# Deformable layer: 13 groups of shifts, five pair sums merged on GpSimd, eight projections, and the far-event chain laid on other shifts

## The chip, the cores and the metric

The kernel is one program on one NeuronCore of a Trainium2 chip. The metric is the device time of one execution in microseconds. The engines are TensorE (PE, with its weight loads PEld), VectorE (DVE), ScalarE (ACT), GpSimd (POOL) and SyncE (SP), which issues most DMAs. They run side by side and meet at semaphores.

## The reference, cut to what matters

The input is x, (4, 128, 64, 64) in float32. A deformable convolution layer is followed by a Mamba block, an attention and expert layer, a second attention and a last expert layer. Only the first layer is touched. It computes:

```
val = xf @ w_value + b_value                       # xf: group-normed x, P = 4096 pixels, C = 128
om  = (xf @ w_off + b_off).reshape(N, P, G=8, 32)  # 9 taps: offsets y, x and a mask
for the four corners of each sample point:
    acc += gather(val, corner) * weight(corner) * valid(corner)
out = (acc * mask).sum(over 9 taps) @ w_out + b_out
out = batchnorm(out);  x += out * sigmoid(out)
```

An offset may point anywhere. Most are small: a sample point then lies within one pixel of its tap, so the gather is a sum over 25 shifts (dy, dx in -2 to 2) of the value image, each with a weight that is a product of two hat functions. The few points beyond ("far events", up to 128 in an image) are found, gathered and added by themselves.

## The kernel before

`deform_near` (L146) works in 16 units: four images (b = 0 to 3) times four units of 8 rows in each half image. A tile is 128 x 1024 (two halves of 512 pixels). In each unit t runs over the 25 shifts, which fall in 9 classes (a class has one product of a y hat and an x hat).

- GpSimd multiplies hats by the mask (`mask_hat`, L378) and forms the tap weights of a class (L426) in a ring of 5 slots. A slot is free when the last shift of its old class is spread. It also adds the finished unit to x (`add_out`, L384) and issues the indirect DMAs of the far events (L393, L399).
- TensorE spreads the tap weights of shift k over the channels (`spread_shift`, L859: four 36x64 matmuls, shown as 8) into one of three PSUM pairs. Behind some shifts it puts other items in the same ring (`prepared`): "o" offsets of unit U + 4 (L808), "v" values (L817), "c" steps of the far-event chain (L823 to L848).
- VectorE multiplies the pair by the shifted values (`product`, L495). The first product of a group goes to SBUF (`near_weighted`, three places), the others stay in PSUM and are added to it (`add`, L506). Groups have 3, 3, 3, 3, 3, 3, 3, 2 and 2 shifts: 25 products, 16 additions, 9 projections.
- TensorE projects a finished group with w_out into `near_out_sum` (L879), two shifts behind the group's last. Ahead of a unit's last projection stands the event pair (L871). The first product of a group waits until the group three before it is projected.
- ScalarE evaluates the offsets (L660, L661), the values (`keep_values`, L673), the hats of the next unit (L694 to L712, at t = 14), and the gate (`bn_gate`, L730) once the last projection of a unit is done. It runs its items in order, the gate first.
- VectorE also finds the largest offsets of unit U + 4 (`find_far`, L514 to L517, at t = 17), and carries the chain: `rank_far` (L521 to L528), `select_far` (L534 to L539), `locate`, `corners` (L557 to L577), `gather_sum`, `event_values`. In the last unit of an image it ranks and selects for the next, in the first unit it does the rest.
- SyncE spills offsets to DRAM and reloads them in the order in which its code is written.

The order on every engine is the order of the code; nothing reorders it. A wait holds everything behind it on its engine.

## Time and profile before

| | |
|---|---|
| median of 3 runs | 7284.67 us (7283.68 to 7285.45) |
| profiled execution | 7285.44 us, span 7283.6 us |
| busy in the span | PE 5758.8, PEld 2032.5, DVE 5812.3, ACT 5316.8, POOL 1443.2 us |
| the layer at hand | from about 50 us to 1165 us, 16 units |
| mean granted TensorE clock | 0.918 of full speed |

### The profile page before, as it was taken

How to read it: one execution, taken by the hardware profiler on the slowest of the kernel's cores; microseconds unless marked ns; L12 is line 12 of the kernel's file. 1: busy time of each engine (PE TensorE's matmuls, PEld its weight loads, DVE VectorE, ACT ScalarE, POOL GpSimd, SP SyncE). 2: the span in 40 equal slices, each digit the busy share in tenths (PEclk: the TensorE clock that was granted, in tenths of full speed). 3: DMA queues.
4: the chain of work that ended last, by engine and by line, in shares of the span. 5: the costliest groups of instructions: out<-in, count | busy, mean ns of one | idle time of the engine just before them, and what ended most of it. 6: DMA issues, size and time to landing. Idle time of an engine off the chain costs nothing. (4 is left out here: it accounts for less than half of the span.)

```text
span 7283.6 us, 89413 instructions
## 1 busy us (share of the span) xinstructions
PE 5758.8 (79%) x32962; PEld 2032.5 (28%) x32962; DVE 5812.3 (80%) x12374; ACT 5316.8 (73%) x3820; POOL 1443.2 (20%) x1695
## 2 busy tenths in 40 slices
PE   7887886788769998977767777887778787778787
PEld 2222222344324443422211222222222222222223
DVE  7888887676557765888777788989889898889996
ACT  3333322455545553579999999999999999999996
POOL 3444441000136654620000000000000000000002
PEclk7888987888879998989999999999999999999998
DMA  3111100100000000000000000000000000000000
GB/s 120 53 42 48 53 19 11 30 24 24 12 9 1 1 1 4 1 7 1 1 1 1 1 1 1 1 1 1 12 1 1 1 1 12 1 1 1 1 1 24
DMA packets 45167, 95.26 MB, mean 13 GB/s; under 512 B 7863, under 2 KB 9657, under 8 KB 43578
## 3 DMA queue, kind: packets, MB, share of 16 engines
q1 hardware_dynamic: 43834, 88.43, 3.7%
q8 instruction: 267, 4.37, 0.2%
q0 software_dynamic: 896, 1.06, 0.1%
q14 instruction: 170, 1.39, 0.1%
HBM read 39.13 MB, written 33.55 MB: 10 GB/s over the span
## 5 line engine op out<-in xcount | busy, mean ns | idle before, releaser
L2814 ACT ACTIVATE aa_tanh<-aa_tanh 128x4096 f32<-128x4096 f32 (+5 forms) x1120 | 3671.0, 3367 | 24.0 <-DVE aa_tanh L2994 23.9
L2994 DVE TENSOR_SCALAR aa_tanh<-aa_f_times,aa_g_bias 128x1024 f32<-128x1024 f32 (+18 forms) x5120 | 2983.2, 643 | 476.6 <-PE aa_scores L2860 470.5
L2860 PE MATMUL aa_scores<-aa_tanh,aa_w_spread 128*32 128x512 f32 (+8 forms) x18432 | 2164.8, 583 | 808.3 <-ACT aa_tanh L2814 803.9
L2860 PEld LDWEIGHTS aa_scores<-aa_tanh,aa_w_spread 128*32 128x32 f32 x18432 | 581.0, 112 | 2237.0 <-ACT aa_tanh L2814 1119.6
L2874 PE MATMUL aa_out_sum<-aa_weights,aa_normed 128*128 128x512 f32 (+3 forms) x1152 | 640.7, 640 | 60.4 <-DVE aa_weights L3003 57.7
L2782 POOL TENSOR_SCALAR aa_group_normed<-x_rows,norm_scale,aa_shift_plus 128x128 f32<-128x128 f32 x96 | 93.2, 982 | 2411.2 <-PE aa_turned L2901 1766.7
L859 PE MATMUL near_weights_spread<-near_tap_weights,near_spread_consts 36*64 36x512 f32 x3200 | 442.6, 664 | 76.4 <-DVE near_weighted L506 36.4
L2085 PE MATMUL qa_out<-qa_hidden_rows,qa_weights_in 128*128 128x512 f32 x1024 | 475.4, 607 | 0.0
L495 DVE TENSOR_TENSOR near_weights_spread<-near_weights_spread,near_values 128x1024 f32<-128x1024 f32 x256 | 314.1, 1227 | 109.7 <-PE near_weights_spread L859 109.0
L879 PE MATMUL near_out_sum<-near_weighted,near_w_out 128*128 128x512 f32 x576 | 342.0, 724 | 65.8 <-DVE near_weighted L506 65.4
L426 POOL TENSOR_TENSOR near_tap_weights<-near_hat_y_mask,near_hat_x 128x1024 f32<-128x1024 f32 x144 | 339.6, 2372 | 197.4 <-PE near_weights_spread L859 137.9
L2806 ACT ACTIVATE aa_weights<-aa_scores,aa_weights_in 128x1024 f32<-128x1024 f32 (+5 forms) x320 | 312.8, 977 | 89.5 <-PE aa_scores L2860 89.5
L2770 POOL TENSOR_SCALAR aa_normed<-x_rows,norm_scale,aa_attention_shift_plus 128x128 f32<-128x128 f32 x128 | 101.1, 806 | 1162.5 <-PE aa_out_sum L2874 1154.6
L2874 PEld LDWEIGHTS aa_out_sum<-aa_weights,aa_normed 128*128 128x128 f32 x1152 | 182.7, 199 | 524.2 <-issue 416.7
L506 DVE TENSOR_TENSOR near_weighted<-near_weighted,near_weights_spread 128x1024 f32<-128x1024 f32 x256 | 312.7, 1221 | 17.0 <-DVE near_weights_spread L495 0.5
L2447 ACT ACTIVATE L_ffn_weighted<-L_ffn_experts,L_ffn_gates 128x128 f32<-128x128 f32 x640 | 182.8, 369 | 162.2 <-PE L_ffn_experts L2403 161.7
L2037 ACT ACTIVATE qa_hidden_rows<-qa_hidden 128x512 f32<-128x512 f32 x320 | 170.0, 595 | 153.3 <-PE qa_hidden L2076 153.3
L2544 DVE SCALAR_TENSOR_TENSOR x_rows<-L_ffn_experts,L_ffn_gates,x_rows 128x128 f32<-128x128 f32 x640 | 216.8, 346 | 70.8 <-PE L_ffn_experts L2403 59.2
L2403 PE MATMUL L_ffn_experts<-L_ffn_expert_w_centred,L_ffn_normed_T 128*128 128x512 f32 x512 | 250.4, 617 | 20.4 <-DVE x_rows L2544 13.4
L3104 DVE SCALAR_TENSOR_TENSOR x_rows<-aa_turned,aa_gates,x_rows 128x128 f32<-128x128 f32 x768 | 264.0, 344 | 0.0
L2085 PEld LDWEIGHTS qa_out<-qa_hidden_rows,qa_weights_in 128*128 128x128 f32 x1024 | 184.8, 190 | 282.4 <-issue 282.4
L730 ACT ACTIVATE near_bn_out<-near_out_sum,near_bn_shift,near_bn_scale 128x1024 f32<-128x1024 f32 x16 | 19.3, 1205 | 301.3 <-PE near_out_sum L879 301.3
(434 smaller groups left out, 6799.8 us busy)
## 6 DMA issues: line engine op xcount, KB each, us to landing
near_offsets<-near_offset_staged SPq DMA_DIRECT2D x45, 512.0 KB, 3.1
l_taps<-l_scan_in_out SPq DMA_DIRECT2D x256, 64.0 KB, 2.0
x_rows<-in_x SPq DMA_DIRECT2D x4, 2048.0 KB, 15.9
near_offset_y<-near_offsets SPq DMA_DIRECT2D x15, 512.0 KB, 4.1
near_offset_x<-near_offsets SPq DMA_DIRECT2D x15, 512.0 KB
near_mask<-near_offsets SPq DMA_DIRECT2D x15, 512.0 KB, 5.5
out_x<-x_rows SPq DMA_DIRECT2D x3, 2048.0 KB, 6.3
out_x<-x_rows SPq DMA_DIRECT2D x8, 256.0 KB, 2.0
```

The lines of the kernel that those rows point to most:

```text
L426: pool.tensor_tensor(PP[:, n % PR_, :], HY[:, cy, :], HX[:, cx, :], ALU.mult).then_inc(p_ready, 1)
L495: v.tensor_tensor(out.rearrange("p s (r w) -> p s r w", w=WW), w.rearrange("p s (r w) -> p s r w", w=WW), V[:, :, at:at + 8 * VW].rearrang ...
L506: v.tensor_tensor(PR[:, at, :], PR[:, at, :], wp[:, PAIR["s", U, t] % 3, :, :].rearrange("p s n -> p (s n)"), ALU.add).then_inc(added, 1)
L859: last = t.matmul(wp[o:o + 64, r, s, :], e[64 * h:64 * h + 36, :], PP[64 * h:64 * h + 36, n % PR_, s * BANK:(s + 1) * BANK], start=True, s ...
L879: last = t.matmul(acc[:, s, :], WO2[:, s, :], PR[:, gi % 3, s * BANK:(s + 1) * BANK], start=g == 0, stop=g == NGR - 1)
L2085: last = t_.matmul(fo[:, n % 2, :], W2T[:, SET * q + g, :], HR[:, q % 2, g, :], start=q == 0 and g == 0, stop=q == NQ - 1 and g == SET - 1)
L2806: a.activation(ET[:, n % 2, 0:w], sp_[:, n % 2, 0:w], ACT.Exp, bias=B2C).then_inc(e_ready, 1)
L2814: a.activation(TH[:, u % PLACES, 0:length], TH[:, u % PLACES, 0:length], ACT.Tanh).then_inc(th_ready, 1)
L2860: last = t.matmul(sp_[32 * q:32 * q + 32, n % 2, s:e], W2S[:, tt, :], TH[:, p, o + s:o + e], start=tt == 0, stop=tt == 3, tile_position=(0 ...
L2874: last = t.matmul(op[:, s0:(h + 1) * BANK], UN[:, j * P:(j + 1) * P], ET[:, n % 2, s0 - lo:(h + 1) * BANK - lo], start=j == 0, stop=n == c ...
L2994: ins = v.tensor_scalar(TH[:, p, at[q]:at[q] + w - s], FR[:, m % 2, lo + s:CHUNK], GB[:, key:key + 1], None, ALU.add)
L3104: v.scalar_tensor_tensor(x, bank("e", E)[:, e * P:(e + 1) * P], GT_[:, G % 2, c:c + 1], x, ALU.mult, ALU.add).then_inc(sum_step if e < 3 e ...
```

## The change

- Groups: `SIZES` is 1 and twelve times 2. 25 products, 12 additions. `near_weighted` has five places (`NSUM`).
- GpSimd adds the sums of the groups (0,1), (2,3), (4,5), (6,7) and (8,9) pairwise (`merge`). Each pair sum has one projection, groups 10, 11 and 12 one each: eight. They stand behind the shifts `PROJECT_AT` = 8, 12, 16, 20, 24, 26, 27, 28, where 26 to 28 are shifts 1 to 3 of the next unit.
- GpSimd's code now runs over t. A class product is put where its slot comes free, four slots ahead (ring of 4 for 5), so that of the next unit's classes the first four are formed in this unit.
- One mask buffer for two; the mask of the next unit is reloaded by itself (`reload_mask`), ahead of the spills.
- Offsets of U + 4 at t = 6, 8, 10 (9, 11, 13 before), values at t = 2 and 4 (5 and 7), find_far at t = 12 (17), hats at t = 11 (14). Chain: rank 13, select 19 (18, 20), locate 1, corners 7, gather_sum 13, event_values 21 (0, 4, 8, 14).
- find_far drops its cast; rank_far reads the indices as they are and uses scalar_tensor_tensor forms for tensor_scalar ones.

```
-        SIZES = [3] * 7 + [2, 2]
+        SIZES = [1] + [2] * 12
         NGR = len(SIZES)
+        PROJECTED = [(0, 1), (2, 3), (4, 5), (6, 7), (8, 9), (10,), (11,), (12,)]
+        PROJECT_AT = [8, 12, 16, 20, 24, 26, 27, 28]
+        NPJ = len(PROJECTED)
+        MERGES = [z for z in PROJECTED if len(z) == 2]
+        MERGE_AT = [5, 9, 13, 17, 21]
...
+            def merge(U, m):
+                g0, g1 = MERGES[m]
+                group_added(pool, U, g0)
+                group_added(pool, U, g1)
+                at, frm = (U * NGR + g0) % NSUM, (U * NGR + g1) % NSUM
+                pool.tensor_tensor(PR[:, at, :], PR[:, at, :], PR[:, frm, :], ALU.add).then_inc(merged, 1)
...
+            for n in range(PR_):
+                class_product(n)
             for U in range(NU):
+                for t in range(NSH):
+                    if t in CLS_LAST and U * NCC + CLS_LAST.index(t) + PR_ < NU * NCC:
+                        class_product(U * NCC + CLS_LAST.index(t) + PR_)
+                    if U and t == 3:
                         add_out(U - 1)
...
+                    if U and U % 4 == 0 and t == 4:
                         gather_offsets(U // 4)
...
+                    if t in MERGE_AT:
+                        merge(U, MERGE_AT.index(t))
...
-                if first and gi >= 3:
-                    v.wait_ge(proj, 1 + gi - 3 + 1)
+                if first and gi >= NSUM:
+                    v.wait_ge(proj, 1 + projection_of(gi - NSUM) + 1)
...
-            CHAIN_FIRST = {11: rank_far, 13: select_far, 16: locate, 18: corners, 21: gather_sum, 24: event_values}
-            CHAIN_BEFORE = {18: rank_far, 20: select_far}
-            CHAIN_WITHIN = {0: locate, 4: corners, 8: gather_sum, 14: event_values}
+            CHAIN_FIRST = {9: rank_far, 12: select_far, 15: locate, 18: corners, 21: gather_sum, 24: event_values}
+            CHAIN_BEFORE = {13: rank_far, 19: select_far}
+            CHAIN_WITHIN = {1: locate, 7: corners, 13: gather_sum, 21: event_values}
...
-                    if t == 17 and U + 4 < NU:
+                    if t == (16 if U == 0 else 12) and U + 4 < NU:
                         find_far(U + 4)
...
-            def project(U, g):
+            def project(U, i):
...
+                if len(z) == 2:
+                    t.wait_ge(merged, 1 + U * len(MERGES) + MERGES.index(z) + 1)
                 else:
+                    group_added(t, U, z[0])
```

TensorE at the start of unit 6, before: shifts 0 and 1 of the unit, the event pair and the last projection of unit 5, shifts 2 to 4, the first projection of unit 6.

```order
L859 MATMUL near_weights_spread<-near_tap_weights,near_spread_consts 64x512 [waits near_product_ready,near_tap_weights_ready]
L859 MATMUL near_weights_spread<-near_tap_weights,near_spread_consts 64x512 x3
L871 MATMUL near_out_sum<-near_event_at,near_event_out 128x512 [waits near_event_at_ready,near_prep_used]
L871 MATMUL near_out_sum<-near_event_at,near_event_out 128x512
L879 MATMUL near_out_sum<-near_weighted,near_w_out_2 128x512 [waits near_sum_added]
L879 MATMUL near_out_sum<-near_weighted,near_w_out_2 128x512
L859 MATMUL near_weights_spread<-near_tap_weights,near_spread_consts 64x512 [waits near_sum_added,near_tap_weights_ready]
```

The same place after: from shift 2 of unit 6 to shift 4. The projections of groups 11 and 12 of unit 5 stand behind shifts 2 and 3.

```order
L899 MATMUL near_weights_spread<-near_tap_weights,near_spread_consts 64x512 [waits near_sum_added,near_tap_weights_ready]
L899 MATMUL near_weights_spread<-near_tap_weights,near_spread_consts 64x512 x3
L918 MATMUL near_out_sum<-near_weighted,near_w_out_2 128x512 [waits near_sum_added]
L918 MATMUL near_out_sum<-near_weighted,near_w_out_2 128x512
L857 MATMUL near_weights_spread<-x_rows,near_w_value_scaled 128x512 [waits near_product_ready,near_weights_scaled]
L857 MATMUL near_weights_spread<-x_rows,near_w_value_scaled 128x512
L899 MATMUL near_weights_spread<-near_tap_weights,near_spread_consts 64x512 [waits near_product_ready,near_tap_weights_ready]
L899 MATMUL near_weights_spread<-near_tap_weights,near_spread_consts 64x512 x3
L910 MATMUL near_out_sum<-near_event_at,near_event_out 128x512 [waits near_event_at_ready,near_prep_used]
L910 MATMUL near_out_sum<-near_event_at,near_event_out 128x512
L918 MATMUL near_out_sum<-near_weighted,near_w_out_2 128x512 [waits near_sum_added]
L918 MATMUL near_out_sum<-near_weighted,near_w_out_2 128x512
```

The last projection moved two shifts later, and the value pair (behind shift 5 before) stands ahead of it.

GpSimd in unit 5, before: `add_out` among the class products 5 and 6 to 8.

```order
L426 TENSOR_TENSOR near_tap_weights<-near_hat_y_mask,near_hat_x 128x1024 [waits near_spread_done,near_hat_y_masked]
L384 TENSOR_TENSOR x_rows<-x_rows,near_bn_out 128x2x512 [waits near_y_ready]
L426 TENSOR_TENSOR near_tap_weights<-near_hat_y_mask,near_hat_x 128x1024 [waits near_spread_done,near_hat_y_masked] x3
L378 TENSOR_TENSOR near_hat_y_mask<-near_hat_y_mask,near_mask 128x1024 [waits near_hat_y_ready,near_mask_loaded_0]
```

After, in an ordinary unit: `add_out`, the last mask product of the unit, class product 6, the first merge (L446), class product 7, the second merge.

```order
L410 TENSOR_TENSOR x_rows<-x_rows,near_bn_out 128x2x512 [waits near_y_ready]
L404 TENSOR_TENSOR near_hat_y_mask<-near_hat_y_mask,near_mask 128x1024 [waits near_hat_y_ready,near_mask_loaded]
L438 TENSOR_TENSOR near_tap_weights<-near_hat_y_mask,near_hat_x 128x1024 [waits near_spread_done,near_hat_y_masked]
L446 TENSOR_TENSOR near_weighted<-near_weighted 128x1024 [waits near_sum_added,near_product_ready]
L438 TENSOR_TENSOR near_tap_weights<-near_hat_y_mask,near_hat_x 128x1024 [waits near_spread_done,near_hat_y_masked]
L446 TENSOR_TENSOR near_weighted<-near_weighted 128x1024 [waits near_sum_added]
```

The first merge stands three instructions behind one that waits for the gate.

TensorE behind shift 8 of unit 6, after: the first projection waits for the merge (`near_sums_merged`), the second offset pair and shift 9 stand behind it.

```order
L899 MATMUL near_weights_spread<-near_tap_weights,near_spread_consts 64x512 x3
L918 MATMUL near_out_sum<-near_weighted,near_w_out_2 128x512 [waits near_y_ready,near_sums_merged]
L918 MATMUL near_out_sum<-near_weighted,near_w_out_2 128x512
L848 MATMUL near_weights_spread<-x_rows,near_w_off_scaled 128x512 [waits near_prep_used,near_weights_scaled]
L848 MATMUL near_weights_spread<-x_rows,near_w_off_scaled 128x512
L899 MATMUL near_weights_spread<-near_tap_weights,near_spread_consts 64x512 [waits near_product_ready,near_tap_weights_ready]
```

Before, the projection at this place waited for an addition of VectorE two shifts back.

## Rows read from the trace of the kernel before

**Rows 1.** Windows view: units 5 to 8 and 13, and the stage.
```profile
core 0: us, PE busy (x) PEld busy (x) DVE busy (x) ACT busy (x) POOL busy (x), PEclk, DMA share, GB/s
...
447.00:512.10 65.10, 58.38 (x260) 17.50 (x256) 52.94 (x47) 22.02 (x23) 32.16 (x14) 0.87 0.14 49
512.10:573.80 61.70, 55.20 (x260) 16.71 (x256) 52.87 (x47) 22.13 (x23) 28.63 (x13) 0.92 0.16 52
573.80:649.80 76.00, 62.42 (x290) 22.04 (x286) 64.16 (x57) 22.50 (x25) 29.82 (x13) 0.84 0.12 42
649.80:726.90 77.10, 58.62 (x272) 19.54 (x268) 65.46 (x83) 24.42 (x30) 37.50 (x21) 0.87 0.17 45
...
997.00:1052.50 55.50, 47.47 (x244) 14.38 (x240) 48.59 (x44) 15.51 (x16) 30.82 (x14) 0.91 0.09 29
...
50.50:1165.00 1114.50, 939.73 (x4252) 305.01 (x4252) 935.06 (x928) 343.94 (x381) 506.08 (x234) 0.87 0.14 44
```

**Rows 2.** Timeline of VectorE, units 6 and 7: start us, us, instruction, [idle before, releaser].
```profile
554.11 1.22 DVE L514 TENSOR_TENSOR near_offset_size<-near_offset_size,near_event_at 128x1024 f32<-128x1024 f32 x1
...
558.24 1.21 DVE L495 TENSOR_TENSOR near_weighted<-near_weights_spread,near_values 128x1024 f32<-128x1024 f32 x1
...
579.23 1.23 DVE L495 TENSOR_TENSOR near_weights_spread<-near_weights_spread,near_values 128x1024 f32<-128x1024 f32 x1 [1.82 <-PE near_weights_spread L859]
...
582.84 1.22 DVE L495 TENSOR_TENSOR near_weights_spread<-near_weights_spread,near_values 128x1024 f32<-128x1024 f32 x1
584.09 1.22 DVE L506 TENSOR_TENSOR near_weighted<-near_weighted,near_weights_spread 128x1024 f32<-128x1024 f32 x1
585.23 1.23 DVE L495 TENSOR_TENSOR near_weights_spread<-near_weights_spread,near_values 128x1024 f32<-128x1024 f32 x1
```

**Rows 3.** Timeline of TensorE in unit 6.
```profile
542.67 1.88 PE L808 MATMUL near_weights_spread<-x_rows,near_w_off_scaled 128*128 128x512 f32 x4
544.48 2.81 PE L859 MATMUL near_weights_spread<-near_tap_weights,near_spread_consts 36*64 36x512 f32 x24
...
554.25 1.98 PE L879 MATMUL near_out_sum<-near_weighted,near_w_out 128*128 128x512 f32 x4 [1.28 <-DVE near_weighted L506]
...
559.60 1.98 PE L859 MATMUL near_weights_spread<-near_tap_weights,near_spread_consts 36*64 36x512 f32 x8 [2.35 <-DVE near_weighted L495]
...
564.37 3.78 PE L879 MATMUL near_out_sum<-near_weighted,near_w_out 128*128 128x512 f32 x4 [0.39 <-DVE near_weighted L506]
```

**Rows 4.** Timelines of GpSimd and ScalarE in unit 7.
```profile
578.18 1.20 ACT L730 ACTIVATE near_bn_out<-near_out_sum,near_bn_shift,near_bn_scale 128x1024 f32<-128x1024 f32 x1 [17.35 <-PE near_out_sum L879]
...
579.46 2.35 POOL L384 TENSOR_TENSOR x_rows<-x_rows,near_bn_out 128x1024 f32<-128x1024 f32 x1 [1.56 <-ACT near_bn_out L730]
581.77 4.67 POOL L426 TENSOR_TENSOR near_tap_weights<-near_hat_y_mask,near_hat_x 128x1024 f32<-128x1024 f32 x2
...
586.88 1.27 ACT L673 ACTIVATE near_values<-near_weights_spread,near_bias_cols 128x512 f32<-128x512 f32 x2 [7.49 <-PE near_weights_spread L817]
```

**Rows 5.** Windows view, 559.4 to 569.6 in unit 6 (columns as in rows 1).
```profile
559.40:569.60 10.20, 9.20 (x28) 2.39 (x32) 8.27 (x8) 1.40 (x2) 8.16 (x4) 0.50 0.33 98
```

**Rows 6.** Timelines in unit 7 (rank_far) and unit 8 (corners).
```profile
621.06 1.27 DVE L521 TENSOR_SCALAR near_far_is<-near_far_top 128x12 f32<-128x12 f32 x1
622.36 2.26 DVE L523 TENSOR_SCALAR near_far_missed<-near_far_top 128x4 f32<-128x4 f32 x1
...
626.95 0.17 DVE L525 TENSOR_TENSOR near_far_at<-near_far_at,near_far_half 128x12 f32<-128x12 f32 x1
...
627.79 0.59 PE L823 MATMUL near_weights_spread<-near_far_number,consts_sb 128*128 128x1 f32 x2 [9.87 <-DVE near_far_number L528]
...
661.26 4.40 DVE L557 TENSOR_TENSOR near_event_sample<-near_event_base,near_event_offset 128x2 f32<-128x2 f32 x1
```

**Rows 7.** GpSimd's timeline in unit 8; the page's list of DMA issues.
```profile
654.14 0.94 POOL L393 DMA_INDIRECT near_event_offset<-near_offsets,near_event_offset_rows  x1 [0.31 <-issue]
...
near_mask<-near_offsets SPq DMA_DIRECT2D x15, 512.0 KB, 5.5
```

More of the change, by code:

```diff
@@ L246, in adds_until, with projection_of, group_added @@
             return U * (NSH - NGR) + t - group_of(t)
+        def projection_of(gi):
+            U, g = divmod(gi, NGR)
+            return U * NPJ + [g in z for z in PROJECTED].index(True)
+        def group_added(eng, U, g):
+            S = U * NSH + G_FIRST[g + 1] - 1
+            if SIZES[g] > 1:
+                eng.wait_ge(added, 1 + adds_until(S))
+            else:
+                eng.wait_ge(prod, 1 + S + 1)
         def pieces(U):
@@ L271, in prepared @@
                 items.append(("b", 1))
-            if t in (9, 11, 13) and U + 4 < NU:
-                items.append(("o", U + 4, KINDS[(t - 9) // 2]))
-            v = (15, 18) if U == 0 else (5, 7)
+            ahead = (10, 12, 14) if U == 0 else (6, 8, 10)
+            if t in ahead and U + 4 < NU:
+                items.append(("o", U + 4, KINDS[ahead.index(t)]))
+            v = (16, 19) if U == 0 else (2, 4)
             if t in v and v.index(t) < len(pieces(U)):
@@ L277, in prepared @@
             b, u = divmod(U, 4)
-            if u == 3 and b + 1 < NB and t in (19, 23):
-                items.append(("c", b + 1, (19, 23).index(t)))
-            c = (12, 15, 22, 23, 24) if U == 0 else (-1, -1, 10, 12, 16)
+            if u == 3 and b + 1 < NB and t in (17, 23):
+                items.append(("c", b + 1, (17, 23).index(t)))
+            c = (11, 15, 22, 23, 24) if U == 0 else (-1, -1, 16, 19, 24)
             if u == 0 and t in c:
@@ L333, in spill_unit, with reload_offsets @@
                         sp.dma_start(parked[b][kind, :, :, u, :], halves(STG[:, k % 2, :])).then_inc(spilled[k % 2], 16)
-            def reload_unit(U):
+            def reload_offsets(U):
                 b, u = divmod(U, 4)
-                for kind in KINDS:
+                for kind in KINDS[:2]:
                     spills_done(sp, U, kind)
@@ L354, in _ @@
             for U in range(NU):
+                if U and U + 1 < NU:
+                    reload_mask(U + 1)
                 if U + 4 < NU:
@@ L402, in _ @@
+            def merge(U, m):
[6 more added lines that the diff above has]
+                class_product(n)
             for U in range(NU):
-                for cls in range(NCC):
-                    if U and cls == 6:
+                for t in range(NSH):
+                    if t in CLS_LAST and U * NCC + CLS_LAST.index(t) + PR_ < NU * NCC:
+                        class_product(U * NCC + CLS_LAST.index(t) + PR_)
+                    if U and t == 3:
@@ L493, in product @@
                 w = wp[:, PAIR["s", U, t] % 3, :, :]
-                out = PR[:, gi % 3, :].rearrange("p (s n) -> p s n", s=2) if first else w
+                out = PR[:, gi % NSUM, :].rearrange("p (s n) -> p s n", s=2) if first else w
                 v.tensor_tensor(out.rearrange("p s (r w) -> p s r w", w=WW), w.rearrange("p s (r w) -> p s r w", w=WW),
@@ L763, in _ @@
                             keep_bias(1, 1, NB)
-                    if t == 14 and U + 1 < NU:
+                    if t == (14 if U == 0 else 11) and U + 1 < NU:
                         hats_y(U + 1)
@@ L912, in _ @@
                             bias_columns(1, 1, NB)
-            project_if_last(NU * NSH - 2)
-            project_if_last(NU * NSH - 1)
+            for k in range(5):
+                projections_at(NU, k)
 def deform_wide(nc, d, X, consts):
```

116 lines of the change are left out of this document (57 added, 59 removed).

## The prediction, made before the changed kernel was run

> **What bounds the kernel now.** First the windows view, one window for the whole stage and some for single units. The stage, from the first product of unit 0 to the end, is 1114.5 us of the 7283.6 us span; VectorE is busy for 935 and TensorE for 940 of it, GpSimd for 506 [rows 1]. All else in the program is untouched, so the change is worth what it does to the 16 units. An ordinary unit (6 is one) lasts 61.7 us, a unit that ranks far events (7) 76.0, the one that gathers them (8) 77.1, a unit without offsets to prepare (13) 55.5 [rows 1]. Then the timeline of unit 6 by engine. On VectorE a product that opens a group occupies 1.14 us until the next instruction, a product 1.25 and its addition 1.14 (582.84, 584.09, 585.23), which makes 2.39 for the two [rows 2]. On TensorE a shift costs 0.95 (24 matmuls, three shifts, in 2.81) and a projection, an offset pair or a value pair about 1.85 (542.67 to 544.48) [rows 3]. In unit 6 VectorE works 9 x 1.14 + 16 x 2.39 + 3.9 for find_far (554.11 to 558.24 less a little overlap) = 52.4 us, of 61.7: so some 9 us are waits, and these have TensorE as their releaser, such as the 1.82 at 579.23 [rows 2]. TensorE's side shows why: it waits, 1.28 us at 554.25, for the last addition of a group before it projects it, then needs 1.85 + 0.95 before VectorE has a shift again [rows 3]. With an offset pair between, VectorE runs dry. So neither engine bounds alone; they hand three PSUM pairs back and forth, and the projection lies in that loop.
>
> **The change, part by part.** 13 groups for 9: 13 opening products, 12 additions, in place of 9 and 16. VectorE loses 4 x 1.25 us a unit (an opening product pays 1.14 for the 2.39), so 5.0 us a unit, 80 us over 16 units, if it bounded alone. The 0.37 us cast after find_far goes (558.24 shows that 0.3 of it counts) [rows 2]. TensorE loses one projection, 1.85 us. GpSimd gets 5 merges of 2.31 us, the pitch of its 128x1024 tensor_tensor (579.46 to 581.77) [rows 4], 11.6 us a unit, on top of 28.6 in a unit of 61.7 [rows 1]: 40 of about 60, so it does not bound by its sum. The five sum places give a slot back before VectorE comes to it, since product t waits for a projection that stands on TensorE's queue ahead of shift t anyway. The class products of the next unit now start at t = 14 with hats begun at t = 11; I cost that, and four class slots for five, at nothing: a class product is issued at least 6 shifts ahead of its use. The single mask buffer is covered too: SyncE sends the mask of the next unit once mask_hat of t = 4 is done, ahead of the spills in its queue, it lands 5.5 us later [rows 7], and is wanted at t = 14; the offset pairs keep their distance of two shifts, some 4 us or more. If that cover went, GpSimd would hold class products, not TensorE at once.
>
> What is late next is found by walking one unit. Let T be the end of the last projection of the unit before, which now stands behind shift 3. Ahead of T TensorE has bunched work: projections behind shifts 24, 1, 2, 3, the event pair, a value pair. Shift 1 needs the pair that product 23 frees, so it ends 1.3 us before product 0 starts; then 1.85 (projection), 0.95, 3.7 (projection, values), 0.95, 3.7 (event pair, projection): T is 9.8 us after product 0. VectorE waits 1.4 us for shift 3 and 3.5 for shift 4 (ready at T + 0.95).
> Behind T on the other engines: the gate ends at T + 1.2, and only then ScalarE empties the value pair, 1.27 us [rows 4], so shift 5 starts at T + 2.6; GpSimd starts add_out at T + 1.3 (578.18 to 579.46), and behind it in its queue stand mask_hat, class product 6 and the first merge, so the merge starts at T + 1.3 + 3 x 2.31 = 8.2 and ends at T + 10.6. TensorE has shifts 5, 6, an offset pair, 7 and 8 done at T + 8.2, where the first projection waits for that merge: 2.5 us. Everything behind it on TensorE's queue waits too: projection 12.5, offset pair 14.4, shift 9 at T + 15.3. VectorE had ended shift 8 at T + 10.8: 4.5 us dry. Then product 9, 10 to T + 18.9, 11 (0.6 late), 12, find_far 3.7: product 13 at T + 26.7. From there on four shifts cost TensorE 4 x 0.95 + 1.85 = 5.65 and VectorE 7.06, VectorE bounds, 6 x 3.53 = 21.2. Next product 0 at T + 47.9, so the unit is 57.7 us.
> During find_far TensorE runs out of pairs: it idles about 3 us (before: 1.28 and 2.35, and then the clock is at 0.50 of full speed, a shift costs 1.98 and a projection 3.78 [rows 3, 5]). I take it to fall again: four shifts then cost 4 x 1.85 + 3.7 = 11.1 us on TensorE against 7.06; over 10.2 us at 0.50 that is up to 3.6, less the lead of the ring, 2.5 taken. Ordinary unit: about 60 us, 1.7 less than now.
>
> The units with a chain gain more. In unit 7 rank_far is 6.7 us (621.06 until TensorE starts at 627.79) because three of its operations on 12 elements or fewer last 1.27, 2.26 and as long again, back to back, the length of a GpSimd instruction; the one at 626.95 takes 0.17; and TensorE, which has the pair for `ranked` at the head of its queue, idles 9.87 us [rows 6]. After the change rank_far is at t = 13 and the pair at 17, so TensorE does not reach it first; GpSimd waits for the hats at that time, so I take 3 us for rank_far (bounds 1.3 and 7). 57.7 + 3 + 5 (select_far, unchanged) + 3.3 for the lower clock = 69: 7 less. The Trainium skill, page "SBUF — State Buffer", section "Who interferes with whom", says that a VectorE instruction with two SBUF inputs contends with a GpSimd instruction that reads SBUF, and that GpSimd's side is an exclusive lock. It speaks against the new scalar_tensor_tensor forms, which have two SBUF inputs, and against find_far's first operation now that GpSimd has more to do; the rows agree for small operations (4.40 us for 128x2 [rows 6]).
> In unit 8 corners waits up to 4.4 us now; at t = 7 it lies in front of the 4.5 us wait and hides most of itself, but three indirect DMAs (1.3 us apart [rows 7]) stand ahead of the merge, + 3.2; gather_sum and event_values 2.4, three pairs of the chain and the second value pair 2, lower clock 3: 57.7 + 10.6 = 68.3, 8.8 less.
>
> The sum over units, now less then (units not shown are like the shown ones of their kind, but for 0, 1, 12 and 15, the ends, where I take the additions' 5.0 us and a little from the chain): unit 0, 6; 1, 5; ordinary 2, 6, 9, 10, 1.7 each, 7; 5 (a longer low clock now), 4; 3, 7, 11, 7 each, 21; 4 and 8, 17; 12, 7.5; 13 to 15, which have no offset pairs, by the same walk 51.5, so 4, 1 and 5, together 10. That is 77.5 us. Profiled execution 7285.4 us, 0.8 above the median of 7284.7: 7284.7 - 77.5 = 7207 us.
>
> **The rivals.** A: the clock stays up through find_far and the waits. For it: the idle of 1.28 us leaves it at 1.0, the projection behind it takes 1.98 [rows 3]. Then every unit gains 2.5 more: 7207 - 38 = 7169 us.
> B: it falls behind the wait for the merge as well. The idle there is 2.5 us, about the 2.35 behind which it fell in unit 6 [rows 3], but that one came close behind another. The projection, an offset pair and a shift then cost 3.7, 3.7, 1.9 for 4.6 in all: 4.7 us a unit, 15 units, 7277 us; half of them, 7242. The Trainium skill, "TensorE: Matmul & The Clock Gate", section "The HAM clock gate", calls the throttled state the default which activity lifts; by that rule B and the next are the danger.
> C, the other side: the low clock spreads over TensorE's bunched stretch from shift 1 to shift 10 (20 us of dense work at 1.0, and TensorE bounds there, where before it had slack nearly everywhere), because waits for `merged` and for the value pair keep breaking it. Two spells of 10.2 us, 5 us each, on top of the 60: 7207 + 15 x 9.7 = 7352 us. It decides from 5.2 us a unit upward. Against it: the dense stretch itself recovered the clock in 10.2 us in unit 6.
> D: GpSimd's extra 11.6 us of work a unit holds VectorE's two-input operations. At most 2.3 us for find_far and 7 for each rank_far and corners: 35 + 21 us, half of it taken, 7235 us. Below nothing it cannot be.
> E, that the change does not do what it says, is out for the work: 12 additions and 8 projections stand in the program's order. But the gain can vanish where TensorE bounds; that is B and C.
>
> **Chances.** Forecast 0.45, A 0.20, B 0.16, C 0.08, D 0.11. A measurement tells 0.2% from nothing, 14.6 us, so faster is below 7270: the forecast, A, D and a good half of B, 0.85; B's worse half 0.07; C 0.08. The likeliest one's own range is 7185 to 7230; the range over the cases 7160 to 7262.
>
> **What would show it.** Right: an ordinary unit of 58 to 61 us; VectorE's work in it 47; L446 on GpSimd 80 times at 2.35; TensorE idle 2 to 3 us before the first projection of a unit with the merge as releaser, and VectorE dry for 4 us before product 9; no 9.87 us idle for the rank; VectorE without waits from t = 13 on but for a spell at 0.50. Wrong: units of 62 or more with the granted clock below 0.87 (B, C); product or addition longer than 1.23 us; find_far's L514 well above 1.3 us (D); GpSimd late for shift 5 or 7.

## The result, and the profile after

The change made the kernel slower: 7354.47 us, median of 4 runs (7349.02 to 7358.66), against 7285.06 (7283.68 to 7291.20) for the kernel before. The ratio is 1.0092, 95% interval 1.0079 to 1.0105. The forecast was 7207 us, so it missed by 147 us and on the wrong side. The profiled execution has a span of 7347.2 us against 7283.6, at a mean granted clock of 0.913 (0.918 before).

Measured from VectorE's first product of a unit to the next one's, the 16 units sum to 1169.2 us (1108.3 before). So 61 of the 64 us of the span lie in the stage. By unit (us; unit 15 up to its last product):

| unit | 0 | 1 | 2 | 3 | 4 | 5 | 6 | 7 | 8 | 9 | 10 | 11 | 12 | 13 | 14 | 15 |
|---|---|---|---|---|---|---|---|---|---|---|---|---|---|---|---|---|
| before | 112.8 | 68.8 | 61.7 | 76.1 | 77.1 | 65.1 | 61.6 | 76.1 | 77.1 | 62.0 | 61.5 | 76.1 | 70.5 | 55.5 | 52.3 | 54.0 |
| after | 114.4 | 63.4 | 62.2 | 79.4 | 84.7 | 67.4 | 62.2 | 79.3 | 84.7 | 67.4 | 62.1 | 79.3 | 82.7 | 59.7 | 68.5 | 51.8 |
| forecast | 106.8 | 63.8 | 60 | 69 | 68.3 | 61.1 | 60 | 69 | 68.3 | 60.3 | 59.8 | 69 | 63 | 51.5 | 51.3 | 49 |

Units 1, 2, 6 and 10 are near the forecast. In all the units exceed it by 139 us: 84 in the units with the chain (3, 4, 7, 8, 11, 12), 17 in unit 14, 13 in units 5 and 9, 8 each in units 0 and 13, 9 in the rest. So most of the loss is in the chain units and in unit 14.

Windows view of the kernel after: units 5, 6, 7, 8, 13, 14, then the stage. It answers to [rows 1].

```profile
core 0: us, PE busy (x) PEld busy (x) DVE busy (x) ACT busy (x) POOL busy (x), PEclk, DMA share, GB/s
454.10:521.50 67.40, 59.85 (x256) 18.75 (x260) 47.71 (x42) 21.80 (x23) 41.84 (x18) 0.81 0.14 47
521.50:583.70 62.20, 55.00 (x256) 17.00 (x252) 47.54 (x41) 21.91 (x23) 42.49 (x18) 0.89 0.15 51
583.70:662.90 79.20, 62.60 (x286) 23.62 (x282) 58.51 (x52) 22.39 (x25) 42.43 (x18) 0.81 0.12 40
662.90:747.70 84.80, 62.68 (x264) 20.32 (x256) 67.58 (x78) 24.41 (x30) 49.39 (x26) 0.81 0.14 41
1039.20:1098.90 59.70, 51.40 (x240) 14.98 (x244) 43.86 (x39) 15.51 (x16) 42.09 (x18) 0.79 0.09 27
1098.90:1167.40 68.50, 49.07 (x246) 14.84 (x239) 43.58 (x38) 15.51 (x16) 43.74 (x20) 0.80 0.03 8
49.90:1229.00 1179.10, 956.63 (x4188) 314.96 (x4188) 878.84 (x849) 342.26 (x381) 696.38 (x315) 0.81 0.13 42
```

VectorE's work in an ordinary unit fell from 52.9 to 47.5 us, as forecast, but the unit did not get shorter. All of the 5.3 us became waiting. In unit 8 VectorE is busy longer than before (67.6 against 65.5) though it has fewer instructions: some of them are being held. Over the stage VectorE's busy time fell by 56 us, where the 64 additions and the 15 casts that are gone took 93; the other 37 went into operations that last longer now, find_far's first and small ones of the chain. The line view (busy, mean ns; idle before and its releasers) names the new link:

```profile
L918 PE MATMUL near_out_sum<-near_weighted,near_w_out 128*128 128x512 f32 x512 | 320.5, 759 | 38.1 <-POOL near_weighted L446 38.1
L535 DVE TENSOR_TENSOR near_weights_spread<-near_weights_spread,near_values 128x1024 f32<-128x1024 f32 x192 | 235.2, 1225 | 100.6 <-PE near_weights_spread L899 100.3
L446 POOL TENSOR_TENSOR near_weighted<-near_weighted 128x1024 f32<-128x1024 f32 x80 | 188.6, 2358 | 34.4 <-DVE near_weighted L546 27.1 <-issue 7.2
```

TensorE now waits 38 us for GpSimd's merges, less than the 139 that are missing: the rest has to be found elsewhere. The products themselves are as fast as before (1.22 us).

**Unit 14**: timeline of GpSimd, TensorE and VectorE (start, us, engine, instruction, [idle before, releaser]).

```profile
1119.89 2.34 POOL L438 TENSOR_TENSOR near_tap_weights<-near_hat_y_mask,near_hat_x 128x1024 f32<-128x1024 f32 x1
1127.89 0.38 POOL L466 PARTITION_ALL_REDUCE near_far_max_all<-near_far_max  x1 [5.65 <-PE near_weights_spread L899]
...
1135.50 2.33 POOL L446 TENSOR_TENSOR near_weighted<-near_weighted 128x1024 f32<-128x1024 f32 x1 [7.23 <-issue]
...
1137.88 3.78 PE L918 MATMUL near_out_sum<-near_weighted,near_w_out 128*128 128x512 f32 x4 [9.77 <-POOL near_weighted L446]
...
1143.13 1.23 DVE L535 TENSOR_TENSOR near_weighted<-near_weights_spread,near_values 128x1024 f32<-128x1024 f32 x1 [10.33 <-PE near_weights_spread L899]
```

The all-reduce of the flag is recorded with 0.38 us, but GpSimd does nothing else from 1122.2 to 1135.5, 13.3 us. The profile puts the 5.65 us ahead of it down to TensorE; in the kernel before the same idle time (5.63 us) stands there with no releaser, and the same 13.3 us pass from one instruction to the next (1062.8 to 1076.1):

```profile
1060.46 2.36 POOL L426 TENSOR_TENSOR near_tap_weights<-near_hat_y_mask,near_hat_x 128x1024 f32<-128x1024 f32 x1
1068.46 0.38 POOL L416 PARTITION_ALL_REDUCE near_far_max_all<-near_far_max  x1 [5.63 <-issue]
1076.12 4.67 POOL L426 TENSOR_TENSOR near_tap_weights<-near_hat_y_mask,near_hat_x 128x1024 f32<-128x1024 f32 x2 [7.29 <-issue]
```

After the change a merge stands behind it, TensorE's projection waits for the merge, and VectorE waits for the shift behind the projection. In the old kernel only class products stood behind it, and those have slots in reserve: unit 14 took 52.3 us.

**Unit 6**: timeline of GpSimd, then of TensorE, the front of the unit; it answers to the walk and to [rows 3, 4].

```profile
534.84 2.36 POOL L410 TENSOR_TENSOR x_rows<-x_rows,near_bn_out 128x1024 f32<-128x1024 f32 x1 [7.07 <-ACT near_bn_out L770]
537.15 2.36 POOL L404 TENSOR_TENSOR near_hat_y_mask<-near_hat_y_mask,near_mask 128x1024 f32<-128x1024 f32 x1
539.59 2.35 POOL L438 TENSOR_TENSOR near_tap_weights<-near_hat_y_mask,near_hat_x 128x1024 f32<-128x1024 f32 x1
541.90 2.36 POOL L446 TENSOR_TENSOR near_weighted<-near_weighted 128x1024 f32<-128x1024 f32 x1
```

```profile
531.64 1.88 PE L918 MATMUL near_out_sum<-near_weighted,near_w_out 128*128 128x512 f32 x4
533.45 1.09 PE L899 MATMUL near_weights_spread<-near_tap_weights,near_spread_consts 36*64 36x512 f32 x8
536.07 1.95 PE L899 MATMUL near_weights_spread<-near_tap_weights,near_spread_consts 36*64 36x512 f32 x16 [1.53 <-ACT near_values L713]
537.94 3.67 PE L848 MATMUL near_weights_spread<-x_rows,near_w_off_scaled 128*128 128x512 f32 x4
...
544.32 1.98 PE L918 MATMUL near_out_sum<-near_weighted,near_w_out 128*128 128x512 f32 x4 [0.83 <-POOL near_weighted L446]
```

The order of events is the one that the prediction walked through: gate, add_out, mask, class product, merge, projection. T, the end of the last projection of unit 5, is 533.4, so 11.8 us after product 0 (9.8 forecast). The merge starts at T + 8.5 (8.2 forecast) and ends at T + 10.9 (10.6). GpSimd had stood idle for 7.07 us in front of this, waiting for the gate. TensorE waits only 0.83 us for the merge (2.5 forecast), because the offset pair ahead of it took 3.67 us in place of 1.85: the granted clock is 0.50 from 538.1 to 541.5. VectorE is dry for 2.79 us before product 9 (4.5 forecast).

**Unit 7**: timelines of VectorE, then GpSimd, then TensorE and VectorE again; it answers to [rows 6].

```profile
624.09 0.16 DVE L562 SCALAR_TENSOR_TENSOR near_far_missed<-near_far_top 128x4 f32<-128x4 f32 x1
...
636.10 1.10 DVE L574 SCALAR_TENSOR_TENSOR near_far_number<-near_far_rank,near_far_base,near_far_is 128x12 f32<-128x12 f32 x1
637.24 2.27 DVE L575 TENSOR_SCALAR near_far_missed<-near_far_number 128x12 f32<-128x12 f32 x1
639.54 3.85 DVE L578 TENSOR_TENSOR near_event_rows<-near_spread_consts,near_far_number 128x1536 f32<-128x1536 f32 x1
643.42 2.73 DVE L579 TENSOR_REDUCE near_event_row<-near_event_rows 128x128 f32<-128x1536 f32 x1
```

```profile
634.82 2.35 POOL L438 TENSOR_TENSOR near_tap_weights<-near_hat_y_mask,near_hat_x 128x1024 f32<-128x1024 f32 x1 [1.88 <-PE near_weights_spread L899]
637.14 2.34 POOL L446 TENSOR_TENSOR near_weighted<-near_weighted 128x1024 f32<-128x1024 f32 x1
639.44 2.33 POOL L404 TENSOR_TENSOR near_hat_y_mask<-near_hat_y_mask,near_mask 128x1024 f32<-128x1024 f32 x1
```

```profile
648.69 1.99 PE L899 MATMUL near_weights_spread<-near_tap_weights,near_spread_consts 36*64 36x512 f32 x8 [10.27 <-DVE near_weighted L546]
650.61 5.28 PE L869 MATMUL near_weights_spread<-near_far_at,near_event_rows 128*128 128x1 f32 x24
...
658.93 1.23 DVE L535 TENSOR_TENSOR near_weights_spread<-near_weights_spread,near_values 128x1024 f32<-128x1024 f32 x1 [5.72 <-PE near_weights_spread L899]
```

rank_far is short now: its first operation takes 0.16 us, and the next product follows 0.93 us after it began. But select_far is held. L574 ends at 637.20, L575 at 639.51, L578 at 643.39; the first two end within 0.03 us of the end of a GpSimd instruction, the third 1.6 us after one, which is nearly its own length. In the kernel before, the same three took 0.23, 0.17 and 1.76 us. Meanwhile TensorE runs out of PSUM pairs, idles 10.27 us, comes back at 0.5 of full speed (eight matmuls of a shift in 1.99 us) with 24 matmuls of the chain in hand, and VectorE is dry for 5.72 us.

### The profile page after: what moved, and what is told of

It reads as the page before. It is cut to its first block and busy times, and to the rows that moved or that the text cites. A ratio compares the mean times of both kernels' runs of the same rounds, so it can differ in the third digit from the quotient of the medians.

```text
span 7347.2 us, 89313 instructions
## 1 busy us (share of the span) xinstructions
PE 5759.6 (78%) x32898; PEld 2039.5 (28%) x32898; DVE 5756.4 (78%) x12294; ACT 5315.4 (72%) x3820; POOL 1622.7 (22%) x1775
## 5 line engine op out<-in xcount | busy, mean ns | idle before, releaser
L899 PE MATMUL near_weights_spread<-near_tap_weights,near_spread_consts 36*64 36x512 f32 x3200 | 458.4, 683 | 150.6 <-DVE near_weighted L546 77.4
L535 DVE TENSOR_TENSOR near_weighted<-near_weights_spread,near_values 128x1024 f32<-128x1024 f32 x208 | 252.7, 1220 | 168.7 <-PE near_weights_spread L899 168.2
L918 PE MATMUL near_out_sum<-near_weighted,near_w_out 128*128 128x512 f32 x512 | 320.5, 759 | 38.1 <-POOL near_weighted L446 38.1
L535 DVE TENSOR_TENSOR near_weights_spread<-near_weights_spread,near_values 128x1024 f32<-128x1024 f32 x192 | 235.2, 1225 | 100.6 <-PE near_weights_spread L899 100.3
L2444 PE MATMUL L_ffn_experts<-L_ffn_expert_w_centred,L_ffn_normed_T 128*128 128x512 f32 x512 | 250.7, 618 | 20.3 <-DVE x_rows L2585 13.2
```

The source lines that it names most:

```text
L535: v.tensor_tensor(out.rearrange("p s (r w) -> p s r w", w=WW), w.rearrange("p s (r w) -> p s r w", w=WW), V[:, :, at:at + 8 * VW].rearrang ...
L899: last = t.matmul(wp[o:o + 64, r, s, :], e[64 * h:64 * h + 36, :], PP[64 * h:64 * h + 36, n % PR_, s * BANK:(s + 1) * BANK], start=True, s ...
L918: last = t.matmul(acc[:, s, :], WO2[:, s, :], PR[:, (U * NGR + z[0]) % NSUM, s * BANK:(s + 1) * BANK], start=i == 0, stop=i == NPJ - 1)
L2444: last = t_.matmul(ep[:, t % 2, h, :], UT[:, t // CK % 2, t % CK // 4, (t % 4) * P:(t % 4 + 1) * P], EWC[:, 4 * h:4 * h + 4, :].rearrange( ...
```

## The experiments

The ratio of each is against the kernel before in the same session; the changed kernel itself stands at 1.0092.

**The all-reduce of the flag, out of the way of a merge.**

```
-                    if U == NU - 2 and t == 7:
+                    if U == NU - 1 and t == 22:
```

> The changed kernel with GpSimd's partition_all_reduce (for the far flag) moved from unit 14, t = 7, to unit 15, t = 22. Theory Q (GpSimd's queue: what stands ahead of a merge there is paid by TensorE): in unit 14 TensorE waits 9.77 us for the merge behind it, VectorE 10.33; unit 14 falls from 68.5 to about 57, the whole from 7354 to about 7342 us. Theory C (the low clock on TensorE's bunched stretch is what costs): unit 14 changes by under 4 us.

7341.52 us, ratio 1.0083 (1.0065 to 1.0102). Unit 14 falls from 68.5 to 55.4 us, 13.1 us, as long as GpSimd stood still there. All others stay within 0.1 but for unit 15, which is 3.1 us longer (54.9). 10 us by the trace; the interval of the times alone would not resolve it.

**add_out behind the first merge.**

```
-                    if U and t == 3:
-                        add_out(U - 1)
...
+                    if U and t == 5:
+                        add_out(U - 1)
```

> The changed kernel with add_out moved on GpSimd from t = 3 to behind the first merge (t = 5), so that the first merge no longer stands behind an instruction that waits for the gate. Theory Q: the wait before product 9 (step from product 8 to 9: 5.27 us in unit 6, 2.9 of it wait) goes, 2.5 us in 13 units: about 7320 us. Theory C: TensorE bounds the front half of a unit anyway by its bunched items, so the wait reappears elsewhere: under 10 us less, 7345 or more.

7308.05 us, ratio 1.0036 (1.0022 to 1.0051): 0.56% gained, about 41 us, the most that any single edit of the changed kernel gave. TensorE's wait for merges fell from 38.1 to 20.3 us, unit 6 from 62.2 to 58.0, unit 5 from 67.4 to 62.3. In unit 6 product 9, the first behind the wait for the merge, starts 25.1 us after product 0, where it took 27.6 (521.62 to 549.18) in the changed kernel:

```profile
510.28 2.35 DVE L535 TENSOR_TENSOR near_weighted<-near_weights_spread,near_values 128x1024 f32<-128x1024 f32 x2
...
535.40 1.23 DVE L535 TENSOR_TENSOR near_weighted<-near_weights_spread,near_values 128x1024 f32<-128x1024 f32 x1 [1.89 <-PE near_weights_spread L899]
```

That is 2.4 of the 4.2 us. Another 1.5 is won between products 16 and 17, where the spell at half clock is 3.4 us long in place of 6.8. So an instruction that waits for ScalarE's gate, put ahead of the merge, was dear; part of what the edit gave may have come by way of the clock (0.84 over the stage for 0.81), and the runs do not part the two.

**The old places, with the merges kept.** Offset and value pairs, find_far, hats and chain at their old shifts, and GpSimd's indirect DMAs two and four shifts earlier to fit (the code is cut):

```
-            CHAIN_BEFORE = {13: rank_far, 19: select_far}
-            CHAIN_WITHIN = {1: locate, 7: corners, 13: gather_sum, 21: event_values}
+            CHAIN_BEFORE = {18: rank_far, 20: select_far}
+            CHAIN_WITHIN = {0: locate, 4: corners, 8: gather_sum, 14: event_values}
...
-                    if t == (16 if U == 0 else 12) and U + 4 < NU:
+                    if t == 17 and U + 4 < NU:
```

> The changed kernel (13 groups, merges, eight projections, new order of GpSimd) with the places of before for the offset, value and chain pairs, find_far, the chain's steps on VectorE and the hats; the indirect DMAs one or two steps earlier on GpSimd to fit. Theory P (the places are at fault: the chain's steps now meet GpSimd's merges and empty the ring): units 7 and 8 come back from 79.3 and 84.7 to at most 77, the whole to about 7290 or below. Theory M (groups and merges are at fault wherever the rest stands): 7340 or more.

7415.98 us, ratio 1.0186 (1.0169 to 1.0203). Much worse: the theory that the new places cost the time fell. The line view of this kernel:

```profile
L918 PE MATMUL near_out_sum<-near_weighted,near_w_out 128*128 128x512 f32 x512 | 327.5, 774 | 118.0 <-POOL near_weighted L446 117.9
```

TensorE waits 118 us for merges. GpSimd waits 126 us for the hats of y in front of its mask products (36.5 in the changed kernel), and the merges stand behind these. The new places are what makes the merges bearable; which of them does it, this run does not say, as all moved at once.

**The new places alone, on the kernel before.** The same edit the other way round, without the moves on GpSimd.

> The kernel before with the new places only: offsets at 6, 8, 10, values at 2 and 4, find_far at 12, hats at 11, chain at 13, 19 and 1, 7, 13, 21. Theory P: slower than before by 20 us or more, since the chain and the value pair stand badly. Theory M: within 10 us of before or faster, since TensorE no longer sits 9.87 us before the rank pair.

7307.57 us, ratio 1.0036 (1.0022 to 1.0050). Units 3, 7 and 11 become 84 to 86 us (76 before), the ordinary ones stay, unit 12 gets shorter (65.6 for 70.5). Here rank_far, still in its old form, is held at its new shift (12.15 us from its product to the next). So the places cost something without the new forms, and gain only with the merges.

**The value pairs at their old place.**

```
-            v = (16, 19) if U == 0 else (2, 4)
+            v = (16, 19) if U == 0 else (5, 7)
```

> The changed kernel with the value pairs of units 1 to 15 behind shifts 5 and 7, as before, in place of 2 and 4. Theory Q: in unit 6 VectorE's wait for shift 3 (2.3 us of the 4.72 step) goes, and that for shift 7 (1.9 of 4.34), which stands behind ScalarE's late reading of the value pair; some of it comes back as the value pair now falls among the offset pairs. 2 us a unit in 12 units: about 7330 us. Theory C: no change beyond 10 us, 7345 or more.

7343.40 us, ratio 1.0080 (1.0063 to 1.0096). In unit 6 the steps from products 2 and 6 to the next fall by 1.8 and 1.3 us, but the one from product 8 to 9 goes from 5.3 to 9.5 us (2.5 of it work). Product 9 starts 27.3 us after product 0, against 27.6: the wait moves to the merge, for which TensorE now waits 58 us in all (38 before the edit). The gain is not resolved by itself.

**TensorE kept at work during find_far.** The spreading of shift 15 is done four times over in units 1 to 11, which changes no result:

```
-                    spread_shift(U, k)
+                    spread_shift(U, k, 4 if 0 < U < 12 and k == 15 else 1)
```

> The changed kernel with the spread of shift 15 done four times over in units 1 to 11 (same result into the same pair), in the 3.25 us in which TensorE idles during find_far; extra work 2.85 us a unit that fills the idle. Theory C: the granted clock no longer falls in unit 6 at t = 14 to 17, the step from product 16 (4.06) goes to 2.4, and the spell from t = 22 is also rarer: 2 to 4 us a unit, 7315 to 7330 us. Theory Q: the fall of the clock is a consequence and costs little, at most 1.7 us a unit: 7335 to 7354.

7351.74 us, ratio 1.0095 (1.0078 to 1.0112): no gain. In unit 6 the step from product 16 to 17, behind find_far, is 1.7 us shorter and the spell at half clock there is gone, but a shorter one comes at products 18 to 20. The step from product 8 to 9 is 3.4 us longer. TensorE's rows in front of product 9 show why:

```profile
522.92 1.98 PE L848 MATMUL near_weights_spread<-x_rows,near_w_off_scaled 128*128 128x512 f32 x4
524.83 2.28 PE L899 MATMUL near_weights_spread<-near_tap_weights,near_spread_consts 36*64 36x512 f32 x16
529.30 2.71 PE L918 MATMUL near_out_sum<-near_weighted,near_w_out 128*128 128x512 f32 x4 [2.19 <-POOL near_weighted L446]
```

Here the offset pair ran at full clock (1.98 us for 3.67), and TensorE then waited 2.19 us for the merge in place of 0.83. Product 9 starts 27.8 us after product 0, no sooner than without the edit. At this place GpSimd's queue sets the time, not the clock.

**GpSimd held while VectorE does select_far, corners and find_far.** Three waits on GpSimd, in the chain units only:

```
+                    if U % 4 == 3 and U + 1 < NU and t == 20:
+                        pool.wait_ge(sel_ready, 1 + U // 4 + 2)
+                    if U and U % 4 == 0 and t == 6:
+                        pool.wait_ge(corners_ready, 1 + U // 4 + 1)
+                    if U and U % 4 == 0 and U + 4 < NU and t == 13:
+                        pool.wait_ge(ev_done, 1 + U + 5)
```

> The changed kernel with GpSimd made to wait: for select_far before the class product of t = 20 (units 3, 7, 11), for corners before the one of t = 6 and for find_far before the merge of t = 13 (units 4, 8, 12). Theory S (VectorE's operations with two SBUF inputs stand still while GpSimd computes): select_far from 9.9 to 4.9 us, the first operation of corners from 3.88 to 0.2, find_far's first from 5.19 to 1.2; 5 us in each of three units, 6 to 8 in each of the others: about 7320 us. Rival: these stretches are hidden by other waits, under 10 us less in all.

7333.23 us, ratio 1.0065 (1.0048 to 1.0082), about 20 us gained by the medians; the intervals overlap by a little. In the trace the six chain units are 18 us shorter together, and units 13 to 15 lose 12 of it again. VectorE's timeline of this kernel in unit 7, the same four instructions:

```profile
634.55 0.22 DVE L580 SCALAR_TENSOR_TENSOR near_far_number<-near_far_rank,near_far_base,near_far_is 128x12 f32<-128x12 f32 x1
634.80 0.17 DVE L581 TENSOR_SCALAR near_far_missed<-near_far_number 128x12 f32<-128x12 f32 x1
635.01 1.76 DVE L584 TENSOR_TENSOR near_event_rows<-near_spread_consts,near_far_number 128x1536 f32<-128x1536 f32 x1
636.81 2.72 DVE L585 TENSOR_REDUCE near_event_row<-near_event_rows 128x128 f32<-128x1536 f32 x1
```

With GpSimd idle they have their old durations again: 4.9 us for the four, against 10.0. That GpSimd's work stretches them is shown. VectorE's dry spell behind them is 5.72 us as before, so it is not due to the held operations. In unit 8 the holds moved the trouble on: corners and find_far are shorter by 3.1 and 4.0 us, but gather_sum, now beside the delayed GpSimd work, is longer by 7.6.

**Four together** (flag late, add_out behind the merge, values at 5 and 7, GpSimd held).

> The changed kernel with four edits: the flag's reduction in unit 15, add_out behind the first merge, value pairs behind shifts 5 and 7, GpSimd held as in the run before. If the causes add up, 7354 - 13 - 46 - 24 - 34 = 7237 us, below the kernel before (7281 to 7285). If they share one wait, 7270 to 7300. Theory C: 7290 or more.

7257.51 us, ratio 0.9966 (0.9951 to 0.9980): faster than the kernel before. 1.26% gained on the changed kernel, where the four alone give 0.09 + 0.56 + 0.12 + 0.27 = 1.04%; the difference lies within the intervals.

**And the last projections apart.** One projection at a time behind neighbouring shifts, the last one a shift sooner:

```
-        PROJECTED = [(0, 1), (2, 3), (4, 5), (6, 7), (8, 9), (10,), (11,), (12,)]
-        PROJECT_AT = [8, 12, 16, 20, 24, 26, 27, 28]
+        PROJECTED = [(0, 1), (2, 3), (4, 5), (6, 7), (10,), (8, 9), (11,), (12,)]
+        PROJECT_AT = [8, 12, 16, 20, 23, 24, 25, 27]
```

> The kernel with four edits, and the last projections apart: group 10 at 23, groups 8 and 9 at 24, 11 at 25 (shift 0 of the next unit) and 12 at 27, for 24, 26, 27, 28. Theory B (the bunched items of TensorE at the start of a unit bound it there: the step from product 3 is 4.58 us in every version so far, 3.4 of it wait): the step falls to about 2, 2 us a unit: 7230 us. Theory Q: VectorE's dry time moves to the next wait for a merge or the clock: within 8 us of 7257.

7220.79 us (7217.53 to 7228.02), ratio 0.9913 (0.9896 to 0.9930). **The best version**, 65 us below the kernel before in its session, and 0.53% (some 38 us) below the version with the four edits: projections that crowd the start of a unit on TensorE are a cost of their own. Its ordinary units take 54.4 to 56.7 us, unit 7 68.9, units 13 and 14 50.0 and 51.4. Unit 8 still takes 79.4; 8.8 of it pass from product 1 to 2, where `locate` now runs beside GpSimd's instructions (5.0 in the changed kernel).

**gather_corners at t = 7 for 10**, on top.

```
-                    if U and U % 4 == 0 and t == 10:
+                    if U and U % 4 == 0 and t == 7:
                         gather_corners(U // 4)
```

> The same, and the indirect DMAs of the corners' rows at t = 7 on GpSimd for t = 10. Their data is what VectorE waits for at t = 13 in units 4, 8 and 12 (step 9.94 us, 7.2 of it wait). Theory Q: 5 to 7 us less in each of the three units, 18 less than the run before it. Rival: the wait is hidden by TensorE's empty ring: under 6.

7235.95 us, ratio 0.9929 (0.9912 to 0.9945): 15 us worse where 18 better was expected; the intervals overlap. VectorE's timeline of the version before it shows why little could come of it, unit 8:

```profile
655.03 1.98 DVE L630 TENSOR_SCALAR near_event_rows<-near_event_rows,near_event_weights 128x128 f32<-128x128 f32 x1 [1.74 <-DMA near_event_rows<-in_x_tokens,near_event_corner_rows]
657.05 5.19 DVE L632 SCALAR_TENSOR_TENSOR near_event_rows<-near_event_rows,near_event_weights 128x128 f32<-128x128 f32 x3
662.27 0.23 DVE L633 COPY near_event_rows<-near_event_weight 128x128 f32<-128x128 f32 x1
```

Only 1.74 us there are a wait for the DMA. The other 7.2 are four small operations that run while GpSimd works through the mask product and two class products (654.57 to 661.7) that had been held up.

**The filler of find_far on top of that.** The edit of the sixth experiment.

> The same again, and shift 15 spread four times over in units 1 to 11 so that TensorE has no idle in find_far. Theory C (low clock): the step from product 16 falls from 3.8 to 2.4 and nothing comes back: 15 us less. Theory Q: the extra TensorE work and a fall of the clock elsewhere eat it, as in the single test (7352 against 7354): within 8 us.

7240.51 us, ratio 0.9939 (0.9922 to 0.9955). No gain again.

**No merges**: the four mends, but 13 projections of single groups.

```
+        PROJECTED = [(g,) for g in range(13)]
+        PROJECT_AT = [3 + 2 * g for g in range(13)]
...
+        MERGE_AT = []
```

> The kernel with four edits, without merges: 13 groups, 13 projections, each three shifts behind its group's last or only shift. GpSimd does 11.6 us less in a unit, TensorE 5 x 1.85 = 9.3 us more. Theory Q (a merge is late because of GpSimd's queue, and else cheap): TensorE's work of 46.3 + 9.3 = 55.6 us bounds at 60 to 62 a unit: 7300 us or more. Rival M (the hand-over to GpSimd is what costs): 7257 us or less.

7297.62 us, ratio 1.0016 (1.0006 to 1.0026), against 0.9966 with merges: 0.5%, some 36 us. An ordinary unit takes 65.2 us; TensorE's projections cost 450.2 us (316.8 with merges) and VectorE waits for TensorE. This edit also spreads the projections evenly, so what the merges alone are worth it does not say exactly.

## Why the prediction was wrong

**Right.** VectorE's work in a unit (47.5 us, 47 forecast); behind T the walk of unit 6 (the start and the end of the merge, the value pair's wait at shift 5: 1.53 us); the 9.87 us for the rank gone; rank_far short, though 0.9 us and not 3. From T to the next product 0 unit 6 takes 50.4 us, and the walk with its 2.5 us for the clock has 50.4. The unit came out at 62.2 instead of 60 because T itself is 2 us late: shift 1 ends 0.6 us after product 0 and not 1.3 before it. That products and additions stay at 1.22 us beside GpSimd's extra work was right too. Two signs that the prediction named were off even here: TensorE idles 0.83 us before the first projection, not 2 to 3, and units 5 and 9 take 67.4 us at 0.81 of full clock, its sign for rivals B and C.

**The step that failed first: "GpSimd ... so it does not bound by its sum".** True, and it answers the wrong question. GpSimd's sum is 42 us of 62. What changed is its place: the old kernel's GpSimd fed a ring with slots in reserve and could stall 13.3 us in unit 14 unnoticed. Now TensorE waits for each of its merges, so every wait in GpSimd's in-order queue ahead of a merge is TensorE's and then VectorE's wait: the gate ahead of add_out, the all-reduce (13 us in unit 14, which the walk took for a unit like 13), the offsets' DMA issues. The all-reduce I missed altogether. The wait behind the gate was in the walk, so in the ordinary units it is no part of the miss; but I never asked what its place costs, and moving one instruction gave about 41 us.

The same in unit 12, VectorE's and TensorE's timelines after:

```profile
982.68 4.85 DVE L597 TENSOR_TENSOR near_event_sample<-near_event_base,near_event_offset 128x2 f32<-128x2 f32 x1 [3.25 <-DMA near_event_offset<-near_offsets,near_event_offset_rows]
```

```profile
982.96 3.78 PE L918 MATMUL near_out_sum<-near_weighted,near_w_out 128*128 128x512 f32 x4 [3.81 <-POOL near_weighted L446]
```

The offset DMAs are issued (977.06 to 980.5) behind a late class product and ahead of the merge. corners waits for the DMA and is then held by GpSimd, TensorE waits for the merge. Forecast for the unit 63, measured 82.7.

**The second: the chain units, 69 and 68.3 us forecast.** "select_far, unchanged" was the error: its cost is not its own. By the rows, unit 7 is an ordinary unit (62.2) + 0.9 for rank_far + 10.0 for select_far + 5.7 for the dry spell behind = 78.8, of 79.3. The forecast had 57.7 + 3 + 5 + 3.3. In unit 8 corners' first operation takes 3.88 us (0.24 with GpSimd held), find_far's first 5.19 where it takes 1.22 in unit 7, and the last of `locate` 2.40 where it took 0.22 before: 9.8 us of the 16.4 by which the unit exceeds the forecast. This is rival D; I bounded it by 56 us in all and took it at 0.11. Units 3, 4, 7, 8, 11 and 12 exceed the forecast by 84 us together. How much of this is contention alone and how much the merge waits stays open: the holds do not part them cleanly, since they move GpSimd's work too (20 us gained net). The Trainium skill, "SBUF — State Buffer", section "Who interferes with whom", has the rule (two SBUF inputs contend with a GpSimd instruction that reads SBUF); the trace agrees, L578 3.85 us for 1.76, and the products, which have one input in PSUM, are not touched. I had the rule in hand and applied it to the operations that the change edits, not to those that it moves beside a GpSimd with more to do.

**The clock.** Rival C gave 7352 us, and 7354 came. The number agreed by chance. C had two spells of 10.2 us at half clock between shifts 1 and 10 and 9.7 us more in each of 15 units; unit 6 has one spell of 3.4 us there (538.1 to 541.5) and is 2.2 us over the forecast, and the large losses are in units 3, 4, 7, 8, 11, 12 and 14. The granted clock is lower (0.81 over the stage, 0.87 before), and this costs something, as the offset pair of unit 6 shows; but where it was lifted in front of the merge, the wait for the merge took the gain. The filler stood in find_far, behind the stretch that C speaks of, so it is no full test of C. What the low clock costs by itself stays open: unit 5 (0.81) takes 67.4 us and unit 6 (0.89) 62.2 with the same kinds of work, but the rows do not say whether the low clock or the longer waits come first. The run without merges had the highest clock of all in the stage (0.92) and was not the fastest.

**Where the expected gain went.** It is there once the waits are out: the best version has 68.9 us in unit 7, 50.0 and 51.4 in units 13 and 14 (forecast 69, 51.5 and 51.3), less than 60 in the ordinary ones, and 7221 us in all. Its time is near the forecast, but for a kernel whose GpSimd queue is ordered for TensorE's sake and whose last projections stand apart; that the totals meet is luck, since unit 8 is 11 us over its forecast and the ordinary units 3 to 7 under.

## What to carry to other kernels

When work is given to an idle engine, its busy sum is the lesser question. Walk its in-order queue: whatever waits or disappears ahead of the new item (a gate, a collective, DMA issues) becomes a wait of whoever consumes the item, so put the new item first and the patient ones behind. And price the operations that will now run beside a busier GpSimd by how long GpSimd's instructions last, above all the small ones with their inputs in SBUF.

## What the runs showed of the hardware

- A small VectorE operation with its inputs in SBUF, beside back-to-back GpSimd instructions, ends when one of those does: L574 (128x12) 1.10 us, L575 2.27, with GpSimd held 0.22 and 0.17. L575 is a tensor_scalar, with one input tensor, and is held like the others. Longer ones end later by nearly their own length: L578 (1.76 us by itself) 1.6 us after the end of a GpSimd instruction, L554 (1.22) 1.1 us after. A held operation can sit through two GpSimd instructions: L554 started at 710.56 and took 5.19 us, with GpSimd's at 709.96 and 712.29.
- The 0.38 us of PARTITION_ALL_REDUCE is not its cost: from the end of GpSimd's instruction before it to the start of the next 13.3 us pass, in the kernel before and in the changed one alike.
- Merging two sums of 128x1024 on GpSimd takes 2.36 us and saves TensorE a projection (1.98 us at full clock, 3.78 at half). With GpSimd's queue in order, 5 merges a unit over 16 units were worth some 36 us against one projection for each group.
